# The turns of five lines of jobs in another order on every engine

## The reference

```
x = x + L0_attn(norm(x))    # spiking attention: q, k, v through four threshold steps, softmax over 16 heads
x = x + L0_ffn(norm(x))     # linear layers with inputs and weights rounded to 4-bit floats in blocks of 16
x = x + L1_attn(norm(x))    # four Mamba layers: conv over 4 tokens, silu, h = exp(dt*A)*h + dt*B*u, y = C*h
x = x + L1_ffn(norm(x))     # 128 -> 512, two 512x512 layers with gelu, 512 -> 128
x = x + L2_attn(norm(x))    # causal linear attention, 16 heads, chunks of 128
x = x + L2_ffn(norm(x))     # 8 experts of 128 -> 512 -> 128, top 1 by a gate
x = x + L3_attn(norm(x))    # a decaying causal filter over the tokens, gelu, a projection, a norm
x = x + L3_ffn(norm(x))     # dense layer, and 512 retrieved experts: top 8 of 8 x 8 product keys
```

## Time and profile before

| | |
|---|---|
| median of 3 runs | 1997.54 us (1991.67 to 2001.71) |
| profiled execution | 1997.59 us |
| span of its instructions | 1995.8 us |
| mean granted TensorE clock | 0.838 |
| busy: PE / DVE / ACT / POOL | 77% / 81% / 66% / 61% |
| instructions | 27915 |
| DMA | 170.15 MB, 31% of 16 engines' time in the kernel's queue |

### The profile page before, as it was taken

The page is one execution under the profiler, slowest core; times in us unless marked ns, Lnnn a source line. Parts: engine busy times, 40 slices in busy tenths (PEclk is TensorE's granted clock), DMA queues, the critical chain, the costliest instruction groups (busy, mean ns, idle before and its releaser), DMA issues.

```text
span 1995.8 us, 27915 instructions
## 1 busy us (share of the span) xinstructions
PE 1535.3 (77%) x9225; PEld 1079.8 (54%) x9225; DVE 1614.2 (81%) x2548; ACT 1317.8 (66%) x2677; POOL 1212.9 (61%) x1667
## 2 busy tenths in 40 slices
...
GB/s 179 1 64 68 88 60 86 84 65 94 108 110 99 123 107 96 64 65 1 112 112 102 113 79 128 96 88 40 121 131 121 140 101 65 61 30 75 111 17 6
DMA packets 84592, 170.15 MB, mean 85 GB/s; under 512 B 9440, under 2 KB 14944, under 8 KB 84064
## 3 DMA queue, kind: packets, MB, share of 16 engines
...
## 4 chain that ended last, share of the span: by engine, by line
DVE 23%; PE 23%; ACT 12%; issue 6%; POOL 4%; DMA 3%; SPq 1%; DVEq 0%; ACTq 0%; POOLq 0%
DVE m L1027 8%; DVE dtuB L1019 4%; ACT m L1005 3%; PE ps L1435 3%; PE ps L1725 3%; PE ps L1443 2%; PE ps L1282 2%; PE ps L1153 2%; DMA m<-m 2%; POOL m L1038 1%; ACT L344 1%; PE ps L1293 1%; PE ps L944 1%; ACT o L371 1%; DVE o L1586 1%
## 5 line engine op out<-in xcount | busy, mean ns | idle before, releaser
L1038 POOL TENSOR_TENSOR m<-m 128x256 f32<-128x256 f32 x1024 | 908.2, 922 | 181.2 <-DVE m L1027 178.5
L1027 DVE TENSOR_TENSOR_SCAN m<-m,dtuB 128x1024 f32<-128x1024 f32 x256 | 584.2, 2282 | 23.7 <-ACT m L1005 5.6
L1005 ACT ACTIVATE m<-m,Aneg 128x255 f32<-128x255 f32 x1024 | 427.9, 496 | 40.3 <-DMA m<-m 30.8
L1019 DVE TENSOR_TENSOR dtuB<-m 128x1024 f32<-128x1024 f32 x256 | 345.2, 1348 | 16.9 <-DMA m<-m 9.0
L1402 ACT ACTIVATE o<-ps,w_mo 128x256 f32<-128x256 f32 x256 | 114.2, 470 | 116.9 <-PE ps L1435 115.5
L1051 PE MATMUL ps<-m,w_const 128*32 128x256 f32 x2048 | 165.7, 434 | 21.3 <-POOL m L1038 21.0
L1435 PE MATMUL ps<-o 128*128 128x256 f32 x512 | 155.8, 416 | 21.2 <-DVE X L1379 9.2
L361 POOL TENSOR_TENSOR o<-o,mhalf 128x2 f32<-128x2 f32 x64 | 21.0, 328 | 229.3 <-DVE o L355 229.1
L1443 PE MATMUL ps<-o 128*128 128x128 f32 x1024 | 136.8, 288 | 12.4 <-ACT o L1402 10.2
L1153 PE MATMUL ps<-o 128*128 128x256 f32 x512 | 132.9, 411 | 16.9 <-ACT o L1122 9.4
L1443 PEld LDWEIGHTS ps<-o 128*128 128x128 f32 x1024 | 129.3, 201 | 24.8 <-issue 10.4
...
## 6 DMA issues: line engine op xcount, KB each, us to landing
m<-m SPq DMA_DIRECT2D x256, 256.0 KB, 4.9
...
o<-in_mox SPq DMA_DIRECT2D x128, 256.0 KB, 3.2
...
```

Source lines behind the costliest of these rows:

```text
L1005: op = e.activation(dA[at % NA][:, j, 1:CH], R[q][:, h * CH + 1:h * CH + CH], ACT.Exp, scale=Aneg[:, l, 4 * g + j:4 * g + j + 1])
L1019: e.tensor_tensor(dtuB[:, :, :], bc(R[q][:, (2 + h) * CH:(3 + h) * CH].unsqueeze(1), 4, CH), Br[k % 2], ALU.mult).then_inc(S.dve, n.tick(f ...
L1027: e.tensor_tensor_scan(flat(G[at % NG]), flat(dA[at % NA]), flat(dtuB[:, :, :]), 0.0, ALU.mult, ALU.add).then_inc(S.dve, n.tick(f"s{g}"))
L1038: op = e.tensor_tensor(part, part, Cr[k % 2][:, j:j + 1, :], ALU.mult)
```

## The change

Only `ORDER` differs. Every line has the same turns with the same instructions, waits and semaphores; every engine takes them in another order. How far the two texts are apart:

| engine | turns | at another place | furthest move | pairs of turns that changed sides |
|---|---|---|---|---|
| SP | 577 | 337 | 12 | 358 |
| PE | 1314 | 618 | 11 | 546 |
| DVE | 1381 | 527 | 8 | 417 |
| ACT | 1356 | 725 | 12 | 692 |
| POOL | 494 | 78 | 7 | 57 |

The texts run over 8 to 12 lines an engine. Here are SP's and POOL's in full and the first lines of the others:

```diff
     "sp":
-        "uf2s6fs2f3s8f2s4fs9f2sfs2f3s8f2s8f2s2f2s6f2s8f2as2asf2s5a5fafbab2a2s8fbf3bs6b4s2b2a2f3as2as2as2as2afa2fsas2afs3a2"
-        "s2ba3bf2sb2s3bs3b3fsb2f2bfb2s3bs2bsbs6fs2f2s4fs5f2s3fs2fsafs3a3f2afasas2as4a3saf3b3s6bs2b2f2bsfs2bs5b4af2a2fa4s3"
-        "as2a2s2asa4b3fafs6b2fsb2sb6fs2fsb2s2bs2fs2f2a4s2fa2s3a6s7f2s3b4fb2fbfbs2fbs2abs4b2a4faf2s2as5a2sf2s3afs2as3ba2b2"
-        "a2f3b2s7b2asb2fb3f2s2bsbs5b2f2s8fa12b11a3ba8ba2b4a2b4ab8a",
+        "uf2s4fs4f3s8f2s6fs2fs8f4s6fs2f2s4fs5fs3fs4f3s7fsfa2s3fs2as2fa4saf2a2bs3as2b2s3fb2f2bs4fs3b3sb2a2f2as4a2sfas2a2sa"
+        "f3s2a2s3a2sbs2a2baf2b2s3b3fs4bsbfb2fb2s6bs2fb2s7f3s3fsf2s5f2s7fsa4f3a3s4bs2a2s2a3f3b2s5bs3b2f3s2b2s3bs3b3a3f2afs"
+        "a2s4a2s3a5ba2fb2afs6b3sbsfbfb5s5bsbsbf2s2a3sas2f2safa4sa3s5fs3fsfb4sb3f3bs2b2s4as2ab2a3faf2s6as2a3f3s3as4bsbaba2"
+        "faf2s3bsbs3b3sab3f2bfbs7b3s3fs3f2s3a12b12a11ba2b4a2b2ab10a",
     "pe":
-        "a6ua5ub2a5babababa2b2abababab6ababab4a4b2afafb2afbfafa2b4a5ba2fabfa2fa2f2sba2b3a2b2sbabfb4f2sbaf2bafb2sfb5fa2f2a"
...
+        "a11u2b2a5ba2bababab2abababab6ababab4a3babafafb3fafafab3aba5b2a2fafa4f3asab4abab2sb2fb2abfafsf2b2fab2sbf2ab3fabf2"
...
     "dve":
-        "a3u2a5ubu2b7a11bafab2fb2a2ba5b5fb2sfs2fs5bsbs2bsbsb3fs8fsf2s2as8a2fafasaf2s6bs2asa3sasfsa2s3ababa2safabfabfsbs9b"
...
+        "a6ua2u3bub7a11bafab2fb3a6bab4fb2sfs4fsbsbs3bs2b2sb2fs8fsf2s2as8a2f2asaf2sas8aba3sasfsa2s3ababa2safba2fbfsbs9bs3b2"
...
     "act":
-        "a7ua2bau3baba4b2ababa2bab2ab2ab3aba2b4a3bfa2fbfabfb2fafa2fab3sasafabasfba2fs2bsafaf2afsbasb2a2sbsbsab2sbsbf2sbs2"
...
+        "a5ua3ba2u3baba4bababababab2ab3ab2aba2b4a3bfa2fbfabfb2fafafbab2asa2sabafbs2bfafsasa2f3afasb2s2b2asabsb2abs3b2f2s2"
...
     "pool":
-        "ua3b3u3afafba2u2bfbfs5bs5fs6afs6as2bfa2s10fs6b2afs4bs6fs6fsfs7baf2s6bs2afs5as5afsbs3bs4fs7bfs4as2asa2fs8a5fas6ba3"
-        "baba2bs2asaf2as2b4sb2s3b4sb2asf2bs2b2s5fsas6bs2fs4asbs2afs9fas3b2s7fs3bs2afa3s6a4sa2sbf2a3babsa2sbs2as4b4f2b2s4a"
-        "sb4ab2s3bfs5as5fs2bs4fbs8fsbs8fs6as2a3fsbs3ba4ba2bs3a6b3abs2b2s3b3sb3as2ba2b3a4b4a6b6a4b3ab3a",
+        "ua2baub2u4afafba2fb2sfs4bs5fs6afs6as2bfa2s10fs6b2afs4bs6fs7fsfs6baf2s6bs2asfsas8fasbs3bs3fs8fbs4as2asa2sfs7a6fs6"
+        "ba3baba2bs2asafafs2b3sb3s3b4sb2asf2bs2b2s5fsas5bs3fs4asbs3fas8fas2bs3bs6fsbs3afa3s6a4sa2sb2f2a3sba3sbs2as4b4fbfb"
+        "s3as2b4ab2s3bfs6as4fs2bs4fbs8fsbs8fs6as2a3fsbs3ba4ba2bs3a6b2ab2sb2s4b4sb2as2ba2b3a4b4a6b6a4b4ab2a",
```

More of the change, by code:

```diff
@@ L217 @@
[L217 to L225, removed]
-    "dve":
-        "a3u2a5ubu2b7a11bafab2fb2a2ba5b5fb2sfs2fs5bsbs2bsbsb3fs8fsf2s2as8a2fafasaf2s6bs2asa3sasfsa2s3ababa2safabfabfsbs9b"
[L228 to L236, removed]
@@ L237 @@
-    "act":
-        "a7ua2bau3baba4b2ababa2bab2ab2ab3aba2b4a3bfa2fbfabfb2fafa2fab3sasafabasfba2fs2bsafaf2afsbasb2a2sbsbsab2sbsbf2sbs2"
[L239 to L248, removed]
@@ new lines @@
+        "a11u2b2a5ba2bababab2abababab6ababab4a3babafafb3fafafab3aba5b2a2fafa4f3asab4abab2sb2fb2abfafsf2b2fab2sbf2ab3fabf2"
+        "afsa6b2sfa3ba3bfa3f2sbf2a7sab2a2fafabfsaf3absb2f3ababaf3b2sb8sb4fb3fbf2sf2safa2b3af2sf3safa3b2afbafa2fbafb2fabsa3"
+        "bab2safa3fbfbafba2bfafsa6ba2ba2sab2afab2afbfa2fbafbasbfab2a3b2a2ba2safa2ba3b2af2b2afsa2fb3fab3a2sa2b2afa5f2ababa4"
+        "fa2bfafasb4ab7asb4fb2a2b4fabfa2sb2f2bafab2sb4fa2b6f2b2fb2a2fa2fbasba4basba2fb4aba3fafa2fbfbafasa2b2ababa3ba6b2as"
+        "fb3a2f2b2af3b4sb8sb3fa3bafb3fa2bf2absfa3b2a3safba2bf2bfaf2sab4a2b2a2bsabfabaf2af2a3bsfa6b2ababsa2fb2fbfafabafa2f"
@@ new lines @@
+        "a2ba3bsa4b2a2ba2b2aba2baba2bsb3a4b2abafababsfbafbafa2fba2fab2a2b2ab2ababsb2abfb4fab2fb3fbfabfbab2ab2a2b2ab2ab2sb7"
+        "a2b3saba2fa2f2bfaf2a3babsaba2b3a2bsa2fa2b2a3fab2abfbf2asa4fba3b2a5b3asa2fb2abf2babfabfafasb3a2basb2a2fabfa2bfasa2"
+        "bfafafba2sb2afba2ba3bf2b2a2f2b2sfb2abab3a3sbfbaba2fabfab2fbab2fbafbsa2b3a2b7sa2fb2ab3fbfb2fb2fabsfb2ab5ab3sbafb5"
+        "a2fabfa2fa2f2bsa3ba3b2sb2a3fb2a6baba4b4a2basa2b2a3b2sa2bfa3bab2a3b2a3ba3babababab2ababa5baba2b2aba2b2aba2b3a2b3a"
+        "b3a2ba2bababa4baba3bab2ab2ab3ab4ab2abab3ab2ab3ab2ab5ab7ab5aba2ba4b5a2b2a4b7a3b4a2ba",
```

22 lines of the change are left out of this document (21 added, 1 removed).

## The result

The changed kernel takes 1942.8 us (median of 4, 1940.52 to 1949.36), the kernel before beside it 1997.1 us (median of 4): ratio 0.9734, 95% interval 0.9699 to 0.977, 54 us faster. I had forecast 1983 us and a range down to 1955: the direction was right, the size was not; nearly three quarters of the gain are missing from my sum.

A forecast was written before the change was run, and what follows sets the result against it. No engine was taken as full; the chain of waits changes engine at nearly every step. Terms -8.4 + 1.6 - 53.9 + 46 = -14.7 us took 1997.6 us to a forecast of 1983 us, range 1955 to 2010.

The forecast's parts named there:

- term 3: Whole trace: waits on DVE, ACT, PE and POOL filled by turns moved ahead, 53.9 us less; bounds half and all.
- term 4: Whole trace: waits opened by unready turns moved ahead, 288 us times 0.16 from scan unit 17: 46 us more (17 to 72).
- Term 1: ACT's table loads: 21 fewer, 26.9 us less on ACT, 8.4 us less on the path; bounds 0 and 26.9.
- Term 2: The start, before the scan: PE's first value product about 1 us later, at 31.1 us; sum +1.6 us (-2.8 to +4).
- The tail: Lines a and b alone after the scan, from 1758 us: products nearly in the same order, costed at nothing, 238 us as before.
- Nothing to measure: Rival, whole kernel: the next turn's wait takes back what a filled wait gives; 1993 to 2000 us, chance 0.27.
- Front comes late: Rival, scan units: the front line's turns move back on DVE and delay unit starts; 2008 to 2019 us, chance 0.2.
- The clock rises: Rival, 1770 to 1800 us: busier PE goes to the full clock, 10.5 us less, 1972 us; chance 0.05.

The follow-up runs named there:

- the square: Old and new order, each with score products over 32 or 128 rows, on one chip: old 1999.39 and 1956.14 us, new 1944.22 and 1912.31 us.
- Full rows: Kernel before, old order, with the score products of L0Attn and L2Attn over all 128 rows instead of 32 (another output): 1956.3 us, 0.9792.
- seg_tail: Kernel before with the new order only from 1750 us on, on all five engines: 1993.37 us, 0.9967 (0.9931 to 1.0003).
- new_5: The changed kernel itself, unaltered, run again against the kernel before on the same chip: 0.9724.
- unit21: Kernel before with the new order only from 1130 to 1215 us, where scan unit 21 lies: 1987.09 us, 0.9937 (0.9902 to 0.9972).

## Why the prediction was wrong

**One step that failed: the clock was costed at nothing.** The tail's 32-row products without a pause at half clock were read as "this stretch doesn't rise", and carried to the whole kernel as a chance of 0.05. After, the same products run at full clock. The reading was also narrower than the stretch: in the 30 us from 1770 us on, PE was busy 14.5 us with the 32-row products and 11.7 us with products of 128 rows (L1137, L1138, L1153, L377), nearly all at half clock. My own sign of failure, a granted clock that moves by more than 0.02, came: 0.838 to 0.864 in the profiles, 0.839 to 0.858 in the means of the runs.

What the rise is worth is not settled; four ways, from rows here, differ. Some 11 us come from the square, if its overlap is the clock's. PE's busy time falls by 45.9 us, by my own worth for PE 45.9 x 0.41 = 19 us. Full rows gave 42 us for 0.029 of mean clock, so 0.018 to 0.019 would be 27. And 64 runs of the kernel before on four chips differ among themselves: within a chip, 0.01 more of granted clock goes with 3.2 us less (95% interval 1.3 to 5.0), so 0.018 to 0.020 would be 6. I take 19 for the sum below, 6 to 27 as its bounds. What raised the clock in the new order was not isolated: the clock rose in part with the turns from 530 to 1100 us and with those from 1100 to 1345 us, and not with the tail's.

The rule of the Trainium skill that I had set against the row (TensorE: Matmul & The Clock Gate, "Part 1: The HAM clock gate (the "warmup" mystery)") has the clock go to the full one once TensorE is kept busy. The direction, a higher clock, came; its reason isn't shown here: PE's busy share is 77% before and after, and PE was 100% busy from 1775 us to past 1800 us while the clock stayed at 1.2 GHz until 1801. The rival that I made of it was priced at 10.5 us for one stretch of 30 us, and the kernel had 650 us at half clock, of which 120 are gone.

**The other: the balance of terms 3 and 4, waits filled against waits opened.** With the clock at 19, the loads at 12 and the start at 1 us, 54.3 - 32 = 22.3 us are left for terms 3 and 4 together (14 to 35 by the clock's bounds), where I had 53.9 - 46 = 7.9. If term 3 stood, term 4 was 32 us and not 46, 0.11 of the 288 (19 to 40 us, 0.06 to 0.14), within its bounds. Only the difference was measured, and as a remainder. The share of 0.16 came from one place, and there it was right: 1.3 us worked out, 1.55 measured, and 7.68 with SP's old order for the 8.1. One place doesn't give the mean of hundreds. What the 288 us had to be scaled by was the thing the text named, that the turns which feed the moved ones move too: with SP's and POOL's left behind, 44 of 54 us are lost.

The 40 us by which the sum was short are then about 19 of clock (6 to 27), 14 of terms 3 and 4 (6 to 27, the rest of the clock's), 4 of loads (12 for 8.4, +-13) and 2 to 3 of the start. Which of the first two is the larger stays open. The loads' 12 us came with a lower clock, so a part of them may be counted twice.

**Term 1** was right in its count: 175 loads after against the forecast 175 or so, 77 at L343, ACT 27.7 us less busy. Its share on the path was 0.31 by the chain; 12/26.9 = 0.45 measured, with an interval from none to nearly all.

**Term 2** had the wrong sign. PE's first value product starts at 28.91, not 31.1: I let POOL's norm turn wait for b's statistics until 27.4 and then counted its 0.7 us product (L364) a second time; it ran from 26.87 to 28.15. And the spread itself took 0.77 us in its new place, not the 2.01 of the old one; five profiles of the new order on POOL have 0.76 or 0.77. Why isn't known. The scan's first group starts 1.8 us sooner, in another profile of the same kernel (new_5) not at all. Other runs of the same start differ by 5 us, so only PE's row is told.

**The tail** was costed at nothing and is 17 us shorter: some 8 us come with the order of its turns (seg_tail, one profile each; 7 in the medians, not told from nothing). The rest comes only with the turns ahead of it, and with it the half-clock stretch of 30.7 us is down to 3.4: at 436 against 283 ns, 27 us fewer at half clock are an estimate of 9.6 us. The price that I gave for it was right; that it would change wasn't.

**The rivals.** *Nothing to measure* is out. *Front comes late*: DVE's waits for L913 and L926 together are 11.8 us, before 20.0; for the copies (L1018) 11.3 against 9.0. Front wasn't later. *The clock rises* was right in kind; its price was for one stretch alone, and the forecast's own mechanism runs beside it (unit21: 13 us at an unchanged clock). In the scan's stretch my forecast that DVE's idle time falls by some 15 us was half of what was seen, 32.
